# A six-stage decoder on one core: first stage reordered, its decays worked out beside the convolution, and other tile groups and load order in the int4 feed-forward

## The reference

```python
h = x @ w_down.T + b_down                    # 512 -> 128
xmid = h = gelu(h)
for _ in range(2):                           # _hydra, the same weights twice
    z, xBC, dt2 = split(h @ in_w.T)          # 256, 288 and 2 x 4 columns
    dt_fw, dt_bw = softplus(dt2 + dt_bias)   # forward and backward
    xBC = silu(causal_conv(xBC, 7 taps) + conv_b); xs, Bm, Cm = split(xBC)
    y = shifted forward scan + shifted backward scan + xs * (xs @ fcD_w.T + D)
    yz = y * silu(z)
    h = (yz * rsqrt(mean(yz ** 2) + 1e-5) * norm_w) @ out_w.T
h = xmid + sigmoid(gate1) * xmid + (1 - sigmoid(gate1)) * h
x = layernorm(x + x + h @ w_up.T + b_up)
```

```python
gate = silu(x @ ((gate_w - gate_z) * gate_s))    # 512 -> 1792
up = x @ ((up_w - up_z) * up_s)
x = layernorm(x + (gate * up) @ ((down_w - down_z) * down_s))
```

## Time and profile before

| what | us |
|---|---|
| median of three runs | 1743.25 (1743.17 to 1745.52) |
| the profiled execution, its own time | 1745.5 |
| its span, first to last instruction | 1743.7 |
| first stage: first z taken out | 31.0 |
| first product of layer 0 | 64.1 |
| layer 1 starts (PE L280) | 112.0 |
| first product of layer 1 | 146.7 |
| last output copy of layer 1 (L372) ends | 194.97 |
| last residual addition (L478) ends | 203.6 |
| feed-forward stage: first matmul | 575.4 |
| PE behind the last group and the rows before the tail | 779 |
| last transposed part of its norm | 800 |

### The profile page before, as it was taken

The page is one execution under the profiler, slowest core; times in us unless marked ns, Lnnn a source line. Parts: engine busy times, 40 slices in busy tenths (PEclk is TensorE's granted clock), DMA queues, the critical chain, the costliest instruction groups (busy, mean ns, idle before and its releaser), DMA issues. The chain is left out here.

```text
span 1743.7 us, 28819 instructions
## 1 busy us (share of the span) xinstructions
PE 1555.7 (89%) x10647; PEld 1284.7 (74%) x10647; DVE 916.8 (53%) x1625; ACT 789.6 (45%) x2419; POOL 755.0 (43%) x616
## 2 busy tenths in 40 slices
PE   5788799999998499996899756999999999999968
PEld 3667497888886378875677445888888888888856
DVE  0626620333336588864467743555555555555755
ACT  2131223444444355533899833454545455454520
POOL 4100013444422488852543425555555555554413
PEclk9888899999999799997899878999999999999988
DMA  6100100100010455105000121111010111000001
GB/s 200 37 0 0 36 19 19 38 20 21 9 43 2 169 170 169 37 1 152 1 2 2 50 75 60 49 37 32 30 37 25 37 49 37 28 28 13 1 1 48
DMA packets 63474, 77.74 MB, mean 45 GB/s; under 512 B 13884, under 2 KB 43052, under 8 KB 63340
## 3 DMA queue, kind: packets, MB, share of 16 engines
q1 hardware_dynamic: 60860, 74.36, 13.3%
q0 software_dynamic: 464, 1.32, 0.3%
q10 hardware_dynamic: 2016, 0.27, 0.1%
HBM read 73.85 MB, written 2.10 MB: 44 GB/s over the span
## 5 line engine op out<-in xcount | busy, mean ns | idle before, releaser
L1011 POOL TENSOR_TENSOR xa_rs<-xa_ms,minus_half 128x5 f32<-128x5 f32 x64 | 74.7, 1167 | 156.7 <-DVE xa_ms L1233 156.6
L994 POOL TENSOR_TENSOR xa_prob<-xa_prob,xa_inv 128x512 f32<-128x512 f32 x64 | 66.6, 1041 | 138.4 <-DVE xa_inv L1200 138.4
L617 POOL TENSOR_TENSOR xa_prob<-xa_prob,xa_inv 128x1024 f32<-128x1024 f32 x32 | 60.6, 1892 | 142.3 <-DVE xa_inv L871 142.3
L1178 ACT ACTIVATE xa_prob<-xa_prob,xa_peak 128x128 f32<-128x128 f32 x256 | 99.9, 392 | 42.9 <-DVE xa_peak L1244 42.9
L1228 DVE TENSOR_REDUCE xa_ssq<-xa_qn 128x4 f32<-128x512 f32 x64 | 43.9, 686 | 133.1 <-ACT xa_qn L1164 133.1
L1524 DVE SCALAR_TENSOR_TENSOR ff_acc<-ff_ring,ff_sT,ff_acc 128x512 f32<-128x512 f32 x140 | 100.4, 747 | 21.9 <-ACT ff_acc L1478 11.9
L1428 PE MATMUL ff_ring<-xT_hi,ff_w 128*128 128x512 f32 x224 | 93.1, 416 | 18.5 <-DVE ff_acc L1524 12.2
L83 PE MATMUL xa_rows<-late_o_hi,xa_out_hi 128*128 128x512 f32 x256 | 104.1, 406 | 5.2 <-DVE xtok L1207 5.2
L83 PE MATMUL xa_qp<-late_q_hi,xT_hi 128*128 128x512 f32 x256 | 106.8, 417 | 2.0 <-DVE late_q_lo L1191 2.0
L1906 ACT ACTIVATE sa_work<-sa_work,sa_peak 128x128 f32<-128x128 f32 x256 | 99.1, 393 | 10.1 <-DVE sa_peak L1943 10.0
L1740 POOL TENSOR_TENSOR sa_work<-sa_work,sa_inv 128x1024 f32<-128x1024 f32 x32 | 60.7, 1897 | 97.8 <-DVE sa_inv L1947 97.6
(11 more groups left out here) (386 smaller groups left out, 4885.0 us busy)
## 6 DMA issues: line engine op xcount, KB each, us to landing
xa_raw_q<-in_wq SPq DMA_DIRECT2D x8, 1024.0 KB, 5.7
late_raw_o<-in_wo SPq DMA_DIRECT2D x8, 1024.0 KB, 5.3
ff_dn_q<-in_down_w SPq DMA_DIRECT2D x7, 512.0 KB, 3.6
ff_dn_z<-in_down_z SPq DMA_DIRECT2D x7, 512.0 KB, 4.6
ff_dn_s<-in_down_s SPq DMA_DIRECT2D x7, 512.0 KB, 6.5
pre<-in_wq SPq DMA_DIRECT2D x16, 192.0 KB, 3.2
pre<-in_wo SPq DMA_DIRECT2D x16, 192.0 KB, 3.7
sa_work<-in_w_qkvT SPq DMA_DIRECT2D x3, 1024.0 KB, 8.3
```

Source lines behind the costliest of these rows:

```text
L617: pool.tensor_tensor(prob[:, t % 3, :, :], prob[:, t % 3, :, :], bc(inv[:, t % 3, :], 2, [P, Q, KEYS]), ALU.mult).then_inc(s["norm"], 1)
L994: pool.tensor_tensor(prob[:, u % 2, :, :], prob[:, u % 2, :, :], bc(inv[:, u % 2, :], 2, [P, Q, S]), ALU.mult).then_inc(s["norm"], 1)
L1011: pool.tensor_tensor(rs[:, :], ms[:, :], m.minus_half[:, 0:Q + 1], ALU.pow).then_inc(s["rs"], 1)
L1178: last = act.activation(prob[:, u % 2, h, :], prob[:, u % 2, h, :], ACT.Exp, bias=peak[:, u % 2, h:h + 1], accum_out=total[:, u % 2, h:h + 1])
```

## The change

In `hydra_stage`:

- SP loads w_down and b_down first, then xT in two halves of the columns, each with its own semaphore. The down projection waits for its half alone. The copy to uT is gone; layer 0 reads x_mid.
- The `Fori` loops over layers are written out. PE makes all 8 z/dt matmuls of a layer first, then the convolutions, through four banks instead of two, with the transposes of xs for t - 3 and the skips for t - 5 between them.
- DVE's chain is cut in pieces (`softplus_in`, `softplus_out`, `distances`, `exponents`, `decays`) that stand between the bias additions of the convolution; only `mixing_weights` follows the last. ACT's exponential of the decays stands behind the Silu of t = 5, so ACT changes its table four times in a layer.
- ACT makes the high part of the context in layer 0, POOL the low part.
- Products have three buffers; `halves` adds sources 2 and 3 to 0 and 1, and PE adds six. The transposes of y, the output projection (now with tokens on the partitions, 128 columns), the root's scale on its way out, and the transpose back follow tile by tile, one, three and four tiles behind the sum. norm_w is multiplied into w_out at the start. Each tile has its own mean square (DVE) and root (POOL).
- The residual's doubling stands before layer 0 on DVE, the scaling of x_mid before layer 1.

```diff
+        SUMMED = (0, 1, 4, 5, 6, 7)
         xT0 = m.pre[:, :].rearrange("p (c n) -> p c n", c=KC)
...
-                for c in range(KC):
-                    sp_.dma_start(xT0[:, c, :], io["xT"].rearrange("(c p) n -> p c n", p=P)[:, c, :]).then_inc(ld["x"], 16)
                 sp_.dma_start(w_down[:, :, :], io["w_downT"].rearrange("(c p) n -> p c n", p=P)).then_inc(ld["gelu"], 16)
                 sp_.dma_start(b_down[:, :], io["b_down"].rearrange("(p a) -> p a", a=1)).then_inc(ld["gelu"], 16)
+                for h in range(2):
+                    cols = slice(h * HALF, (h + 1) * HALF)
+                    sp_.dma_start(xT0[:, :, cols], io["xT"].rearrange("(c p) n -> p c n", p=P)[:, :, cols]).then_inc(ld[f"x{h}"], 16)
...
+                def z_and_dt(i, t):
+                    u = uT if i else x_mid
+                    if i:
+                        pe.wait_ge(s["u"], L * i - 1 if t == 0 else L * i)
+                    else:
+                        pe.wait_ge(s["mid_act"], t // 4 + 1)
+                    if t >= 2:
+                        pe.wait_ge(s["z_out"], L * i + t - 1)
+                    pe.matmul(bank[t % 2][:, 0:ZDT], u[:, token(t)], w_zdt[:, :], start=True, stop=True).then_inc(s["z_mm"], 1)
+
+                def conv(i, t):
+                    u = uT if i else x_mid
+                    if t >= 4:
+                        pe.wait_ge(s["c_out"], L * i + t - 3)
+                    first = max(0, TAPS - 1 - t)
+                    for k in range(first, TAPS):
+                        last = pe.matmul(bank[2 + t % 4][:, 0:CONV], u[:, token(t - (TAPS - 1) + k)], w_conv[:, k, :],
+                                         start=k == first, stop=k == TAPS - 1)
+                    last.then_inc(s["c_mm"], 1)
...
+                def mixed_sum(i, t):
+                    n = L * i + t
+                    pe.wait_ge(s["half"], n + 1)
+                    if t >= 2:
+                        pe.wait_ge(s["yz"], n - 1)
+                    for src in SUMMED:
...
+                def project_out(i, t):
+                    n = L * i + t
+                    pe.wait_ge(s["y_T"], n + 1)
+                    if t >= 2:
+                        pe.wait_ge(s["u"], n - 1)
+                    for c in range(2):
+                        last = pe.matmul(bank[t % 2][:, 0:DM], yT[:, t % 2, c, :], w_out[:, c, :], start=c == 0, stop=c == 1)
+                    last.then_inc(s["o_mm"], 1)
...
+                        conv(i, t)
+                        if t >= 3:
+                            turn_xs(i, t - 3)
+                        if t >= 5:
+                            skip(i, t - 5)
+                    for t in range(L - 3, L):
+                        turn_xs(i, t)
+                    for t in range(L - 5, L):
+                        skip(i, t)
+                    for t in range(L + 4):
+                        if t < L:
+                            mixed_sum(i, t)
+                        if 1 <= t < L + 1:
+                            turn_y(i, t - 1)
+                        if 3 <= t < L + 3:
+                            project_out(i, t - 3)
+                        if t >= 4:
+                            turn_u(i, t - 4)
...
+                def silu_xbc(i, t):
+                    act.wait_ge(s["c_out"], L * i + t + 1)
+                    act.activation(xbc[:, t, :], xbc[:, t, :], ACT.Silu).then_inc(s["xbc"], 1)
...
+                def out_rows(i, t):
+                    n = L * i + t
+                    act.wait_ge(s["o_mm"], n + 1)
+                    act.wait_ge(s["rms"], n + 1)
+                    if n >= 2:
+                        act.wait_ge(s["u_tr"], n - 1)
+                    act.activation(u_tok[:, t % 2, :], bank[t % 2][:, 0:DM], ACT.Copy, scale=rms[:, t:t + 1]).then_inc(s["o_out"], 1)
...
-                    act.activation(x_mid[:, h * HALF:(h + 1) * HALF], bank[h][:, :], ACT.Gelu, bias=b_down[:, :]).then_inc(s["mid_act"], 1)
-                for h in range(2):
-                    act.wait_ge(s["mid_act"], h + 1)
-                    act.activation(uT[:, h * HALF:(h + 1) * HALF], x_mid[:, h * HALF:(h + 1) * HALF], ACT.Copy).then_inc(s["u"], 1)
...
+                        silu_xbc(i, t)
+                        if i == 0 and 1 <= t <= KC:
+                            act.wait_ge(ld["ctx"], 16)
+                            act.activation(m.cT_hi[:, t - 1, :], xT0[:, t - 1, :], ACT.Copy).then_inc(s["c_hi"], 1)
+                        if t == 5:
+                            act.wait_ge(s["seg"], i + 1)
+                            act.activation(dec[:, :, :, :, :], dec[:, :, :, :, :], ACT.Exp).then_inc(s["dec"], 1)
+                        if t >= 3:
+                            out_xsT(i, t - 3)
...
+                    for t in range(1, L + 4):
+                        if t < L + 1:
+                            square(i, t - 1)
+                            out_yT(i, t - 1)
+                        if 3 <= t < L + 3:
+                            out_rows(i, t - 3)
+                        if t >= 4:
+                            out_uT(i, t - 4)
 
...
+                def products(i, t):
+                    n = L * i + t
+                    if n >= PRODS:
+                        dve.wait_ge(s["y_mm"], n - PRODS + 1)
...
+                def halves(i, t):
+                    n = L * i + t
+                    dve.wait_ge(s["prod"], n + 1)
+                    x = prod[n % PRODS]
+                    dve.tensor_tensor(x[:, 0:2, :], x[:, 0:2, :], x[:, 2:4, :], ALU.add).then_inc(s["half"], 1)
+
+                def gated(i, t):
+                    n = L * i + t
+                    dve.wait_ge(s["y_mm"], n + 1)
+                    if n >= GATED:
+                        dve.wait_ge(s["y_tr"], n - GATED + 1)
+                        dve.wait_ge(s["ssq"], n - GATED + 1)
+                    dve.tensor_tensor(yz[:, t % GATED, :], bank[2 + t % 2][:, 0:DIN], z_act[:, t, :], ALU.mult).then_inc(s["yz"], 1)
+
...
+                dve.wait_ge(ld["up"], 48)
+                dve.scalar_tensor_tensor(m.xtok[:, :, :], m.xtok[:, :, :], 2.0, bc(b_up[:, :], 1, [P, B, D]),
+                                         ALU.mult, ALU.add).then_inc(s["xres"], 1)
+                for i in range(LAYERS):
...
+                    softplus_in(i)
+                    conv_bias(i, 0)
+                    conv_bias(i, 1)
+                    softplus_out(i)
+                    conv_bias(i, 2)
+                    conv_bias(i, 3)
+                    conv_bias(i, 4)
+                    distances()
+                    conv_bias(i, 5)
+                    exponents()
+                    conv_bias(i, 6)
+                    decays(i)
+                    conv_bias(i, 7)
+                    mixing_weights(i)
+                    for t in range(L + 2):
                         if t < L:
-                            if t >= 2:
-                                dve.wait_ge(s["y_mm"], L * i + t - 1)
-                            dve.tensor_tensor(prod[t % 2][:, :, :].rearrange("p s (h n) -> p s h n", h=NH),
-                                              xbc[:, :, 0:DIN].rearrange("p s (h n) -> p s h n", h=NH),
-                                              bc(mixw[:, t * L * NH:(t + 1) * L * NH].rearrange("p (s h) -> p s h", h=NH), 3,
-                                                 [P, L, NH, HDIM]), ALU.mult).then_inc(s["prod"], 1)
-                        if t:
-                            dve.wait_ge(s["y_mm"], L * i + t)
-                            dve.tensor_tensor(yz[:, t - 1, :], bank[(t - 1) % 2][:, 0:DIN], z_act[:, t - 1, :], ALU.mult).then_inc(s["yz"], 1)
-                    dve.wait_ge(s["ssq"], L * i + L)
-                    dve.tensor_scalar(msq[:, :], ssq[:, :], 1.0 / DIN, 1e-5, ALU.mult, ALU.add).then_inc(s["msq"], 1)
-                    dve.wait_ge(s["rms"], i + 1)
-                    for t in range(L):
-                        dve.tensor_scalar(yz[:, t, :], yz[:, t, :], rms[:, t:t + 1], None, ALU.mult).then_inc(s["yn"], 1)
-                dve.wait_ge(ld["up"], 48)
-                dve.scalar_tensor_tensor(m.xtok[:, :, :], m.xtok[:, :, :], 2.0, bc(b_up[:, :], 1, [P, B, D]), ALU.mult, ALU.add).then_inc(s["xres"], 1)
+                            products(i, t)
+                            halves(i, t)
+                        if 1 <= t < L + 1:
+                            gated(i, t - 1)
+                        if t >= 2:
+                            mean_square(i, t - 2)
```

```diff
 GROUP = 4
-TABLE = [(hb, k) for hb in range(2 * math.ceil(TILES / GROUP)) for k in range(min(GROUP, TILES - GROUP * (hb // 2)))]
+GROUPS = ((0,), (1, 2), (3, 4), (5,), (6,))
+HALVES = 2 * len(GROUPS)
...
-        end = {}
-        mid[25], end[25], mid[26], end[26], mid[27], end[27] = [20, 21], [22], [23], [24], [25], [26, 27]
-        first_unit = [min(n for n, (hb, k) in enumerate(TABLE) if hb == x) for x in range(2 * math.ceil(TILES / GROUP))] + [UNITS]
```

(33 more changed lines are left out.)

286 lines of the change are left out of this document (146 added, 140 removed).

## The result

The changed kernel takes 1713.2 us (median of four runs, 1711.6 to 1714.5) where the kernel before takes 1743.2: a ratio of 0.983, 95% interval 0.981 to 0.985, clear of 1. That is 30 us less, where I had forecast 50.7 less (1692.5, range 1681 to 1707): the direction was right, the size was too large, and the time lies outside the range. On another chip the same kernel stood at 0.981 (0.979 to 0.983). The profiled execution has a span of 1712.7 us, against the 1693.0 of my sum.

The account below looks back on a forecast made before the run. PE was taken as near its limit inside parts but idle at joints, VectorE as bounding the early feed-forward. From the median 1743.25, 38.7 us (first stage) and 12 us (feed-forward) came off: 1692.5 us, range 1681 to 1707.

Parts of the forecast that it names:

- The steady sums: Sums over sources, per tile: PE 3.5 us and VectorE 3.4 us, level, so no faster than before.
- layer 1's projections: From layer start to first product: 29.7 us instead of 34.7, 5 us less a layer.
- sums and output: From a layer's first product to the end of its output: 37 us instead of 47.9, 11 us less a layer.
- the 12 us in the feed-forward: Feed-forward units: both 6.6 us load waits go, ending at 766.4 instead of 779; 12 us less, ends 5 and 18.
- the low part at units 9 and 17: Feed-forward: PE needs POOL's low part of down weights one unit earlier; between nothing and 4 us, 3.6 taken.
- Rival 1: Sums: the SBUF interface makes VectorE the bound, 3.9 us a tile instead of 3.5; about 1700 us, chance 0.17.
- rival 2: Feed-forward stays bound by VectorE and POOL, low-part waits at every large row, only 5 us back; 1699.5, chance 0.13.
- rival 4: Interleaved sums: PE falls to its low clock, 7 us a tile, 56 us more; 1748.5, slower, chance 0.02.
- The head: Kernel start to first z evicted: 21.6 us instead of 31.01, 9.4 us less, with xT's first half landed at 8.5.
- fifth rival: Change does nothing in one place, as the head still waits for late small loads (17 us); 1698.5, chance 0.08.
- Layer 0's projections: First z to first product in layer 0: 31.2 us instead of 33.1, first product at 52.8.
- Four such meetings: Layer 0: VectorE's chain beside POOL's low parts of the context, at most 9.4 us, about 5 slack; 1.5 taken.

Follow-up runs that it names:

- earlier down weights: Changed kernel with the feed-forward's down weights of turns 1 and 2 prepared two units earlier: 1704.3 us, ratio 0.977.
- row part: Changed kernel with xT in four parts of 512 KB instead of two column halves, down projection taken part by part: 1706.1 us, ratio 0.979.
- turn 2 free: Changed kernel with down weights two units earlier and VectorE's subtraction for turn 2 cut to 8 of 256 columns: ratio 0.979, feed-forward 196.7 us.

## Why the prediction was right and wrong

**What held.** The steady sums (3.32 us a tile against 3.5); layer 1's projections, start to first product 30.7 against 29.7, and sums and output 38.4 in layer 0 against 37; 7.4 of the 12 us in the feed-forward, with both load waits gone; and the booking of 3.6 us for the low part at units 9 and 17: 3.3 us, of which the earlier down weights took 2.6 away. Rival 1 fell: the roots do meet the products, but POOL waits. Of rival 2 a part came, in three large rows and not in every one. Two slips changed little: the feed-forward sum gives 12.6 (779 less 766.4) where 12 was booked, and rival 4's clock of 0.50 holds from 100 to 105 us, while from 98 to 109 it was 0.59.

**The head, 7.8 us.** The largest of the steps that failed is "0.26 MB and 1 MB stand ahead of the first half's end, between the second part of xT before (about 6.5 us) and the third (about 9.5): 8.5 us". It landed at 16.3. It counted bytes ahead in SP's own queue and left out the 1 MB of taps in POOL's, which had the larger part of what moved from 2 to 7 us (1.10 MB against 0.42). Measured: 12.4 to 14.4 us from the request for a half behind w_down and b_down, 5.2 for the same half ahead of them; 9.0 against 3.9 for a row part. By the Trainium skill (DMA: Bandwidth & Descriptors, Specifications) transfers want lines of 512 bytes or more for the full rate. b_down's are four bytes; but no run here put w_down ahead without b_down, or the taps behind xT, so which of the three holds xT up stays open. The rows would have warned me: the earlier trace rows had TensorE waiting for a 512-byte load at 17.0. My fifth rival (the head still waits for small loads, until 17 us) comes nearest, priced at 6 us less gain, with a chance of 0.08: too low for a term that rested on one interpolation. But its mechanism is another: the small loads were in at 3.9 us, and TensorE waited for xT.

**Layer 0's projections, 2.9 us.** The step is "Four such meetings cost ... I take 1.5". Moving the low parts away gave 4.5 us between the first convolution and the first product. I had the price per meeting right (2.36 us; measured four of 2.2 to 2.4, which is 8.4 us more than the same steps take alone) and the slack of 5 too: 3.0 us reached TensorE's last skips. What I booked as 1.5 is the difference of the two, 9.4 less 5 = 4.4, taken between that bad end and nothing; the bad end came. The other part, up to 2.0 us at the skips, is TensorE's clock, for which I had booked nothing. The Trainium skill (SBUF — State Buffer, Who interferes with whom) states that the shared port pair is an exclusive lock and that the order of issue decides who blocks; the runs agree: VectorE waited in the chain, POOL's roots in the sums. That is why rival 1, which took the same lock to cost VectorE in the sums, fell.

**The joints, 5.5 us.** In two terms (2.4 and 3.1) I had booked a low clock for the first sum only. The end of layer 0 has it too: the clock falls (0.50 from 99.9 to 101.8 us) while TensorE and ScalarE take turns for the last tiles, and z of layer 1 takes 6.4 us instead of 4.8. In five executions product 0 to product 1 took 65.7 to 66.8 us, my 66.7. There the first gate came 7.4 to 7.5 us behind the first product instead of 8.6, and layer 1 began 36.5 to 36.7 us behind it instead of 38.4; z still took 6.3 us in four of them, 5.0 in one. At the end the eight up-projections took 9.53 us at a granted clock of 0.80, where I had 8.4 for the whole step:

```profile
168.88 1.20 PE L333 MATMUL hy_bank<-hy_w_out,hy_yT 128*128 128x128 f32 x4 [0.50 <-ACT hy_uT L415]
...
170.80 9.53 PE L380 MATMUL hy_bank<-hy_w_up,hy_hm 128*128 128x512 f32 x16
```

Four such passes (the first row) took 0.68 us at 96.8 and at 98.5 us, where the granted clock was 1.00. In which state a joint is caught differs between executions of one program, and I can't say from these runs what decides it.

**The feed-forward, 4.6 us.** The step is the sum of VectorE's work up to unit 8: "11 weight pieces at 0.95 = 10.4, three down subtractions at 1.42 = 4.3". Measured 1.19 us a piece (14.3 for twelve, one more than I counted) and 2.30 a subtraction, so 20.0 us for the 14.7 booked. The means of the earlier trace rows came from a stretch where POOL was busy 62% of the time; now it is 78% (52.97 of 68 us). That the longer steps are meetings with POOL is the likely reason; it was seen in single rows only, and cutting one turn's subtractions gave back 2.0 us. Of the 5.3 us more, 3.3 arrived: TensorE has unit 8 done 62.2 us after the start of the stage, where my sum has 58.9. The 2.2 us for POOL's low part at unit 3, for which I had booked nothing, lie in there too. The units behind took 1.5 us more than I had. The spread of this stage (202.1 and 204.8 for the same code) goes with the clock: after the same wait of 2.58 us the next matmul took 0.50 us in one execution and 0.80 in the other.

**The range.** Every term of the two stages missed on the same side, and no rival held such a sum of small misses: the landing, the lock and the low clock were each priced alone, if at all. In the changed kernel lock and low clock stood together in layer 0, though the kernel with turn 2 free shows the first almost without the second. The range reached 14.5 us above the forecast, and the misses came to 20.7.

## What to carry to other kernels

Before you move a load, look at what each transfer took from request to landing, and don't interpolate it by the bytes of one queue: two small loads put ahead of a large one here went with 5 to 9 us more for it, while another engine's queue moved 1 MB. Let each engine wait only for the load that it reads. Take the price of a shared port from meetings that the new order will have, not from means of the old one, and put the second engine's work where the first is idle: the same four operations cost about 4.5 us in the chain, 5.5 in the sums, and nothing behind them. Behind a wait of TensorE, take the work at the low clock as the bad end of the sum: after the same wait it came in one execution and not in another.

## What the runs showed that I had not expected

- A load of 512 bytes in 128 lines landed 2.7 us after its request as the second in SP's queue, 9.5 us in ScalarE's queue beside four large transfers, and 14.7 behind xT.
- The lock has no side of its own: 64 elements or 4 on VectorE took 2.2 to 2.4 us behind a low part, a root of one element on POOL took 2.53 behind a product. Only a product that met a low part took longer itself, 4.43 instead of 2.28.
- An earlier start of TensorE by 5.9 us, and of z by 0.95, gave nothing at the first product: z then ran mostly at the low clock, 0.82 instead of 0.57 us a matmul.
